# A graph layer on one core: part of the key products in another block, x loaded in pairs, clears spread over the steps, stores and loads on another queue

## What is computed

```python
h = (xn @ W).reshape(-1, 4, 64)                       # graph attention
e = leaky_relu(a_src[src] + a_dst[dst], 0.2)
ex = exp(e - segment_max(e, dst)[dst])
out1 = sigmoid(segment_sum(ex / segment_sum(ex, dst)[dst] * h[src], dst) + bias)
q, k, v = split(xn @ Wqkv)                            # mixer, 8 heads of 32
k = softmax(k, axis=nodes)
context = einsum('bnhd,bnhv->bhdv', k, v)
gate = sigmoid(gelu(LN(xn) @ Wg1 + bg1) @ Wg2 + bg2)
out2 = (q @ context) * gate @ Wproj + bproj
x = x + out1 + out2
x = x + top_k_only(gelu(LN(x) @ w1 + b1) @ w2 + b2)   # weighted by the router
```

## Time and profile before

| | us |
|---|---|
| median of 3 runs | 1721.76 |
| lowest, highest | 1719.15, 1723.86 |
| profiled execution | 1718.96 |
| its span (first to last instruction) | 1717.1 |
| TensorE busy | 1139.1 (66%) |
| VectorE busy | 1041.2 (61%) |
| GpSimd busy | 850.3 (50%) |
| ScalarE busy | 567.4 (33%) |

### The profile page before, as it was taken

How to read it: one execution, slowest core, us unless ns; L and a number is a source line. 1 busy time by engine, 2 the same in 40 slices (tenths; PEclk the granted TensorE clock), 3 DMA queues, 4 the chain that set the end, 5 groups by cost and what they waited for, 6 DMA issues and landing times. The chain is left out here.

```text
span 1717.1 us, 26741 instructions
## 1 busy us (share of the span) xinstructions
PE 1139.1 (66%) x6583; PEld 860.9 (50%) x6583; DVE 1041.2 (61%) x2649; ACT 567.4 (33%) x1372; POOL 850.3 (50%) x881
## 2 busy tenths in 40 slices
PE   5868445654667767666666677676686775766871
PEld 4656333332546546455455555454564654545651
DVE  6735335446666666666656666666575665766757
ACT  4433212120333323333334333333233333333540
POOL 0600444454566566565665565655565655566000
PEclk9989767677788898898888898888888888898995
DMA  7566554443445444444444444444444444445204
GB/s 223 165 164 171 149 155 116 116 120 91 127 119 129 111 128 119 112 126 114 118 128 110 124 125 113 122 120 114 125 117 115 124 114 118 115 118 130 56 1 150
DMA packets 166018, 210.85 MB, mean 123 GB/s; under 512 B 51163, under 2 KB 130587, under 8 KB 165871
## 3 DMA queue, kind: packets, MB, share of 16 engines
q0 software_dynamic: 39984, 110.94, 25.6%
q1 hardware_dynamic: 125991, 99.41, 20.7%
HBM read 165.93 MB, written 44.30 MB: 122 GB/s over the span
## 5 line engine op out<-in xcount | busy, mean ns | idle before, releaser
L734 POOL DMA_INDIRECT ring<-feat_d,idx x832 | 814.8, 979 | 620.5 <-issue 477.1
L1623 PE MATMUL bank<-ring,hot 128*64 128x265 f32 x1664 | 317.8, 529 | 274.9 <-issue 141.3
L1623 PEld LDWEIGHTS bank<-ring,hot 128*64 128x64 f32 x1664 | 174.5, 187 | 400.6 <-issue 318.8
L1248 DVE TENSOR_TENSOR ring<-ring,bank 128x1024 f32<-128x1024 f32 x208 | 239.7, 1214 | 1.8 <-issue 1.4
L1651 PE MATMUL bank<-late,w_s 128*128 128x128 f32 x1568 | 212.2, 294 | 7.2 <-ACT late L1478 7.2
L1651 PEld LDWEIGHTS bank<-late,w_s 128*128 128x128 f32 x1568 | 206.6, 209 | 11.8 <-issue 4.7
L1602 PE MATMUL bank<-w_s,hT 128*128 128x256 f32 x784 | 188.3, 394 | 3.7 <-ACT hT L1485 3.7
L1438 ACT ACTIVATE bank<-diff 128x64 f32<-128x64 f32 x52 | 11.8, 228 | 472.6 <-DVE diff L1235 279.5
L1602 PEld LDWEIGHTS bank<-w_s,hT 128*128 128x128 f32 x784 | 148.7, 195 | 23.3 <-ACT hT L1485 4.3
L1485 ACT ACTIVATE hT<-bank,b_s 128x128 f32<-128x128 f32 x392 | 109.4, 374 | 129.9 <-remote 128.3
L1231 DVE TENSOR_TENSOR ring<-bank,lastT 128x64 f32<-128x64 f32 x52 | 11.7, 225 | 229.4 <-remote 211.3
(11 more groups left out here) (249 smaller groups left out, 1695.9 us busy)
## 6 DMA issues: line engine op xcount, KB each, us to landing
parts_d<-wout SPq DMA_DIRECT2D x208, 66.2 KB
...
lists<-dloc_d SPq DMA_DIRECT2D x104, 128.0 KB
parts_d<-hot SPq DMA_DIRECT2D x50, 265.0 KB
parts<-parts_d SPq DMA_DIRECT2D x49, 265.0 KB
...
```

Of the source, the lines that this page charges most:

```text
L734: pool.indirect_dma_start(out=ring[:, u * TI + q, 0:AW], out_offset=None, in_=feat_d, in_offset=bass.IndirectOffsetOnAxis(ap=idx[:, u, q:q ...
L1248: V.tensor_tensor(feats, feats, ex[:, g * TG:(g + 1) * TG, :].unsqueeze(3) .to_broadcast([P, TG, HEADS, HD]), ALU.mult).then_inc(S("scaled ...
L1623: mm = T.matmul(bank[2 + n][c * WIN:(c + 1) * WIN, 0:SW], hot[:, q, :], ring[:, u * TI + q, 0:SW], start=(j == 0), stop=(j == TG - 1))
```

## The change

- `EARLY` = 23: the first block makes key products only for tiles 0 to 22. The other 26 stand at the start of the last block, where GpSimd gathers the rows of step 0: TensorE (`key_products`), ScalarE (`key_tile`) and VectorE (`maximum_of`).
- The maximum across the partitions, the zeroing of `exp_sum` and the first two subtractions move into step 0 (`MAXIMUM`), ahead of its context chunk. `CHUNKS` become 9, 10, 10, 10, 10 tiles in steps 0 to 4; no context tile stands before step 0.
- x is loaded again in pairs of tiles (four pair slots, eight tiles), by SyncE behind the windows instead of ahead of the breaks.
- 8 tiles of `parts_d` (and a spare one) are cleared in the first block, the other 41 one per step in steps 0 to 49 (`CLEARS`, with a row number made by GpSimd in `clear_i`; nine of the fifty go to the spare tile). `zero` and `rmax` have their own buffers. The fallback block clears all tiles itself.
- `brk_d` is stored once instead of four times, and read with each row repeated for four heads.
- The stores of `brk_d`, `dloc_d` and the targets' sums are issued by ScalarE, in the first block at tiles 32 and 44 and at its end. The loads of Wqkv's parts, w1 and w2 are issued by ScalarE in step 0. In ScalarE's tile the gelu comes ahead of the key copy.
- Features and hidden values are stored in pairs of tiles. The loops of the first block on VectorE, ScalarE and SyncE are written out.
- Turning and centring `wq` moves from the fold in step 4 to step 2 (`PREPARE`). GpSimd makes one more check (that no window reaches rows which are not cleared yet), three operations.

```diff
+CLEARED = 8
+EARLY = 23
...
+brk_d = scratch("brk_d", [NI, GI, GE])
...
+for t in (NT, *range(CLEARED)):
+    clear(t)
+def store(p):
+    n = min(2, NT - 2 * p)
+    sp.wait_ge(S("feat_made"), 2 * p + n)
+    sp.dma_start(feat_d[2 * p * P:(2 * p + n) * P, :].rearrange("(t p) c -> p t c", p=P),
+                 feat_slot[:, 2 * (p % 2):2 * (p % 2) + n, 0:AW]).then_inc(S(f"feat_out{p % 2}"), 16)
+    if p:
+        store_hidden(p - 1)
...
+if 1 <= i <= EARLY:
+    dve.wait_ge(S("keys_kept"), i)
+    if i > 1:
+        dve.wait_ge(S("key_max"), i - 1)
+    V.tensor_tensor(rmax[:, :], rmax[:, :], big[:, i - 1, :], ALU.max).then_inc(S("key_max"), 1)
...
+def body(i):
     act.wait_ge(S("hid_asked"), i + 1)
-    if not known_below(i, 2):
+    if i >= 2:
         act.wait_ge(S("hid_turned"), i - 1)
-    A.activation(sd[:, u, 0:GH], sc[:, u, 0:GH], ACT.Gelu).then_inc(S("hid_made"), 1)
-    if not known_below(i, 1):
-        keep_hidden(i - 1, 1 - u)
-def keep_hidden(i, u):
+    A.activation(sd[:, i % 2, 0:GH], sc[:, i % 2, 0:GH], ACT.Gelu).then_inc(S("hid_made"), 1)
+    if i:
+        keep_hidden(i - 1)
+    if i < EARLY:
+        act.wait_ge(S("keys_done"), i + 1)
+        A.activation(big[:, i, :], bank[4 + i % 2][:, 0:C], ACT.Identity, bias=padneg[:, i:i + 1],
+                     scale=rstd[:, i:i + 1]).then_inc(S("keys_kept"), 1)
...
+bodies(STOPS[2], STOPS[3])
+act.wait_ge(S("breaks_made"), 1)
+act.dma_start(brk_d.rearrange("k g e -> k (g e)"), br_f).then_inc(S("lists_out"), 16)
+act.wait_ge(S("dloc_made"), 2)
+act.dma_start(dloc_d, dl_b).then_inc(S("lists_out"), 16)
+store_targets(0)
+bodies(STOPS[3], TARGETS[2] + 2)
+store_targets(1)
+bodies(TARGETS[2] + 2, NT)
+keep_hidden(NT - 1)
+store_targets(2)
...
+if i < EARLY:
+    if i >= 2:
+        pe.wait_ge(S("keys_kept"), i - 1)
+    for t in range(CT):
+        mm = T.matmul(bank[4 + u][:, 0:C], tile[:, t * P:(t + 1) * P], wk_s[:, t, :],
+                      start=(t == 0), stop=(t == CT - 1))
+    mm.then_inc(S("keys_done"), 1)
...
+x_pair = [xs[:, :, :], sa[:, :, :], sd[:, :, :],
+          hT[:, 4:8, :].rearrange("p a b -> p (a b)").rearrange("p (t c) -> p t c", t=2)]
...
-CHUNKS = [(0, 12)] + [(n, n + 4) for n in range(12, 44, 4)] + [(44, NT)]
-def CONTEXT(f):
-    def two(k, u):
-        for n in range(2 * k + 1, min(2 * k + 3, len(CHUNKS))):
-            f(n, u)
-    return 0, 5, two
+MAXIMUM = lambda f: (0, 1, f)
+CHUNKS = [(0, 9), (9, 19), (19, 29), (29, 39), (39, NT)]
+LOAD_MIXER = lambda f: (0, 1, f)
+PREPARE = lambda f: (2, 3, f)
+CLEARS = lambda f: (0, NI - 2 - NI % 2, f)
+CONTEXT = lambda f: (0, 5, f)
...
+sp.dma_start(brk[:, 1:GE + 1], brk_d.rearrange("k g e -> (k g) e")[bass.ds(row, GI), :].unsqueeze(1)
+             .to_broadcast([GI, HEADS, GE])).then_inc(S("brk_in"), 16)
...
+def load_again(p):
+    n = min(2, NT - 2 * p)
+    if p >= 4:
+        sp.wait_ge(S("renormed"), 2 * p - 6)
+    sp.dma_start(x_pair[p % 4][:, 0:n, :], x.rearrange("(t p) c -> p t c", p=P)[:, 2 * p:2 * p + n, :]
...
+def clear(k, u):
+    first = nc.values_load_multi_w_load_instructions(
+        clear_i[0:1, bass.ds(k + CLEARED, 1)], engines=[mybir.EngineType.SP], min_val=0, max_val=NT * P,
+        skip_runtime_bounds_check_because="multiples of a tile made on the chip")[1]
+    sp.wait_ge(S("idx_made"), 2)
+    sp.wait_ge(S("zeros_out"), 16 * (k + CLEARED + 2))
+    sp.dma_start(parts_d[:, bass.ds(first[0], P), :].rearrange("n p c -> p n c"),
+                 zero[:, 0:SW].unsqueeze(1).to_broadcast([P, 2, SW])).then_inc(S("zeros_out"), 16)
...
-steps(sp, [AHEAD(ahead), MERGE(load_x), CONTEXT(context), AHEAD(breaks_ahead),
-           EDGES(windows), NODE_AHEAD(load_node)])
+steps(sp, [AHEAD(ahead), MERGE(load_x), CLEARS(clear), AHEAD(breaks_ahead), EDGES(windows),
+           CONTEXT(context), NODE_AHEAD(load_node)])
...
+def maximum_of(i, u):
+    dve.wait_ge(S("keys_kept"), i + 1)
+    if not known_below(i, 1):
+        dve.wait_ge(S("key_max"), i)
+    V.tensor_tensor(rmax[:, :], rmax[:, :], keys(i), ALU.max).then_inc(S("key_max"), 1)
+def maximum(k, u):
+    then, settle = chain(dve, "dve_fold")
+    dve.wait_ge(S("max_across"), 2)
+    then(V.tensor_reduce(mg[:, 1, 2:2 + CT], bank[5][:, 0:C].rearrange("p (t n) -> p t n", t=CT), AX_X, ALU.max))
+    settle()
+    for t in range(CT):
+        V.tensor_scalar(sc[:, 0, t * P:(t + 1) * P], ones[:, :], mg[:, 1, 2 + t:3 + t], None, ALU.mult
+                        ).then_inc(S("max_spread"), 1)
+    dve.wait_ge(S("max_across"), 3)
+    then(V.tensor_copy(cmax, bank[6][:, 0:C]))
+    V.memset(exp_sum, 0.0).then_inc(S("constants_kept"), 1)
+    settle()
+    dve.wait_ge(S("constants_kept"), 2)
+    less(0)
+    less(1)
...
-context(0, 0)
+sweep(dve, EARLY, NT, 1, 0, maximum_of)
...
-CONTEXT(context), SUM(sums), MERGE(merge), SUM(normed), FOLD(fold), SEARCH(search)])
+MAXIMUM(maximum), CONTEXT(context), PREPARE(prepare), SUM(sums), MERGE(merge), SUM(normed), FOLD(fold), SEARCH(search)])
...
+def key_tile(i, u):
+    act.wait_ge(S("keys_done"), i + 1)
+    A.activation(big[:, bass.ds(i, 1), :].rearrange("p a c -> p (a c)"), bank[5 + u][:, 0:C],
+                 ACT.Identity, bias=padneg[:, bass.ds(i, 1)], scale=rstd[:, bass.ds(i, 1)]
+                 ).then_inc(S("keys_kept"), 1)
+def load_mixer(k, u):
+    act.wait_ge(S("keys_done"), NT)
+    act.dma_start(wq_s, Wqkv.rearrange("(t p) n -> p t n", p=P)[:, :, 0:C]).then_inc(S("wqv_in"), 16)
+    act.dma_start(feat[:, :, 0:C], Wqkv.rearrange("(t p) n -> p t n", p=P)[:, :, 2 * C:3 * C]
+                  ).then_inc(S("wqv_in"), 16)
+    for o, i in later:
+        act.dma_start(o, i).then_inc(S("ffn_in"), 16)
+def first_renorm(k, u):
+    act.wait_ge(S("max_across"), 3)
+    renorm(0, 0)
...
+def key_products():
+    for i in range(EARLY, NT):
+        if i >= 2:
+            pe.wait_ge(S("keys_kept"), i - 1)
+        for t in range(CT):
+            mm = T.matmul(bank[5 + i % 2][:, 0:C], xnT[:, i, t * P:(t + 1) * P], wk_s[:, t, :],
+                          start=(t == 0), stop=(t == CT - 1))
+        mm.then_inc(S("keys_done"), 1)
+def maximum(k, u):
+    pe.wait_ge(S("key_max"), NT)
+    pe.wait_ge(S("keys_kept"), NT)
+    for t in range(CT):
+        mm = T.transpose(bank[5][:, t * P:(t + 1) * P], rmax[:, t * P:(t + 1) * P], ident[:, :])
+    mm.then_inc(S("max_across"), 1)
+    pe.wait_ge(S("max_spread"), CT)
+    for t in range(CT):
+        mm = T.matmul(bank[6][:, t * P:(t + 1) * P], sc[:, 0, t * P:(t + 1) * P], ident[:, :],
+                      start=True, stop=True)
+    mm.then_inc(S("max_across"), 1)
...
+key_products()
 scores(0, 0)
 steps(pe, [EDGES(turn_scores), FF1(first_ff1), EDGES(turn_maxima), SUM(project), FF1(other_ff1),
-           EDGES(first_sums), EDGES(other_sums), AHEAD(scores_ahead), CONTEXT(context), FF1(ff2),
+           EDGES(first_sums), EDGES(other_sums), AHEAD(scores_ahead), MAXIMUM(maximum), CONTEXT(context), PREPARE(prepare),
+           FF1(ff2),
            FOLD(fold), MERGE(mixer), SUM(turn_normed), SEARCH(search)])
```

282 lines of the change are left out of this document (128 added, 154 removed).

## The result

In the comparison of the two kernels, five runs of the changed one gave 1734.33 us as their median (1730.73 to 1737.92), five of the kernel before 1719.15 us. The ratio is 1.0088 with the interval 1.0060 to 1.0116: **slower by 0.9%**, where 1703 us was forecast.

What follows compares the result with a forecast made beforehand. The 45 equal steps (1203.6 of 1717.1 us) were taken as bound by a chain round the engines, none always busy. Terms -23 - 12.5 + 15 + 2 = -18.5 gave 1700.5 us, 1703 as a median; forecast 1692 to 1714, range 1682 to 1728.

Steps and rivals of the forecast that it cites:

- Products block: First block up to its last store: 26 tiles without key products get cheaper and the store wait shrinks, -23 us.
- Light tiles: Products block: the 26 tiles without key products take 1.5 us each instead of 2.08, 39 us in all.
- the stall: Products block: VectorE's 18 us wait for a feature store shrinks to 5 us of remaining small-row traffic.
- the lists, check and second store: Products block, added costs: third turn of the lists 5 us, VectorE's check 2, second target store 3.
- Head: Start of the last block to first scores: 26 key tiles replace 12 context tiles, 29.6 us instead of 42, -12.5 us.
- Rival (3): Head of the last block: the queue of gathers sets its 42 us, so nothing is saved; 1716 us, chance 0.05.
- milder form: Head: VectorE's maxima run only between gathers, 35 us for 26; 1712 us, no separate chance given.
- Steps 0 to 4: First five steps of the last block: 49 context tiles instead of 37, plus the maximum chain, 183 us, +15 us.
- The term for x: Steps 0 to 4: waits for x tiles to load, 10 us for 49 context tiles (before: 20 for 37).
- Clears: Loop of the last block: one clear per step on SyncE's queue, +2 us in all (0 to 37).
- Rival (4): Loop steps: each is bound by transfers and grows by the clear's 0.83 us, 45 times; 1738 us, chance 0.14.

Runs made afterwards that it cites:

- 1720 kind: Not one run: the kind of chip, or chip condition, on which the kernel before takes 1717 to 1725 us (medians); the first comparison fell on it.
- e4: Changed kernel with all 49 clears in the first block and none in the steps, on the 1394 kind: 1396.95 us, ratio 1.0021 to the kernel before.
- e4b: Changed kernel with all 49 clears in the first block and none in the steps, on the 1720 kind: 1761.90 us, ratio 1.0213 to the kernel before.
- e2b: Changed kernel whose first GpSimd gather waits until all key tiles are kept, on the 1720 kind: 1740.08 us, ratio 1.0091 to the kernel before.
- 1394 kind: Not one run: the other kind of chip, or chip condition, on which the kernel before takes 1393 to 1396 us (medians).
- e7b: Changed kernel with key products, maximum and context tiles placed as in the kernel before, on the 1720 kind: 1735.32 us, ratio 1.0067 to the kernel before.
- e5: Changed kernel with a GpSimd memset behind every fourth gather of steps 0 to 9, on the 1720 kind: 1718.87 us, ratio 1.0003 to the kernel before.

## Why the prediction was wrong, step by step

- **Products block, -23.** Right, and low: -32.5 and -26.2 us on the 1720 kind, -29.6 on the other. Light tiles at 1.46 us (1.5 assumed), the stall 4.2 (5 assumed), and the lists, check and second store together cost less than the 20 us that were added. What took the 18 us away is only in part known. It wasn't the clears: with all 41 back in this block the wait is 4.9 us in e4 and 4.8 in e4b. The three break stores that are gone, the other queue and the later tile changed together, and no run parts them. The Trainium skill, "DMA: Bandwidth & Descriptors", section "Issuing engines are not separate DMA queues", would let the other queue alone save issue time only; no run here shows it.
- **Head, -12.5.** This is the step that failed. It took the earlier trace rows, ScalarE without work for 10.29 us, as "x comes late", and so a burst of key tiles without x was to run freely. The measured head is +13.0 and +13.9 us. The wait was one for TensorE's result (the scaling of an x tile also waits for a bank's context matmul): x was there at 202.1, and the wait for TensorE ended at 213.0. Key tiles depend on the same way from TensorE to ScalarE in each tile, and beside gathers it was up to 19 us long. e2b shows it: 27.7 us without gathers. Their own price, 1.0 us a tile and 29.6 in all, was right where nothing is late: 27.9 us on the 1394 kind. There, too, nothing is gained, since before's head is 21.7 us: +6.2.
- **Rival (3)**, the gathers hold the head, had the right mechanism and the wrong size and chance: not "stays at 42" but 55. Its milder form, VectorE's maxima only between gathers, didn't occur. In the changed kernel a maximum runs inside a gather (timeline, 1720 kind):

```profile
161.38 0.95 POOL L754 DMA_INDIRECT ring<-feat_d,idx  x1 [0.30 <-issue]
...
161.69 0.42 DVE L1131 TENSOR_TENSOR rmax<-rmax,big 128x256 f32<-128x256 f32 x1 [0.51 <-ACT big L1543]
```

  The Trainium skill, "SBUF — State Buffer", section "Who interferes with whom", has a VectorE instruction with two SBUF inputs contend with a GpSimd instruction that reads SBUF. Of `tensor_tensor` the same section says that it wasn't seen to stall a DMA issued by GpSimd, and infers why. The prediction left that out; this trace agrees with it.
- **Steps 0 to 4, +15.** Right in sign; +25.5 and +24.7 on the 1720 kind, +19.7 on the other. 12 more context tiles at 1.1 us and the chain were counted. Not counted: the maximum chain stands beside gathers, and its first hop costs 10 us on the 1720 kind. The term for x was misread as well: in the trace of before, ScalarE's four waits above 3 us ahead of such a scaling in this stretch (5.6, 5.6, 3.4 and 3.6 us) all end with TensorE's update. Of the 10 us above the forecast, the part that is there on the 1394 kind too (+19.7 against +15) has no cause shown.
- **Clears, +2.** The term itself was right within what can be told: 0 (20.54 us a step without, 20.57 with them, on the 1394 kind). Rival (4) came near the measured time, 1738 against 1734, with a mechanism that e4 and e4b refute. Steps 10 to 50 grew by 11.7 and 4.8 us on the 1720 kind for another reason, which stays open; the lag of TensorE's results is the candidate.
- **The sum**: -23 - 12.5 + 15 + 2 = -18.5 forecast; on the 1720 kind -32.5 + 13.0 + 25.5 + 12.8 = +18.8, on the other -29.6 + 6.2 + 19.7 + 4.0 (steps 5 to 50) - 2.4 (end) = -2.1. Even the 1394 kind gives 2 to 4 us of the 18.5, because the head of before was misread as 42 us of work that could be replaced.

**Open**: why steps 0 to 4 and the loop are slower on the 1720 kind in e7b than in before (x in pairs, the order on SyncE's queue and the load of the breaks weren't undone one by one); why the two kinds differ at all; whether the lag in the steps goes without the gathers as that in the head does (e5 and the first and last steps speak for it, but no run on the 1720 kind has its middle steps without them).
